# Blend stage of a two-layer graph network: a block's own h times its softmax weight, from GpSimd to ScalarE

## The chip, the core and the metric

One core of a Trainium2 chip runs the whole kernel in one launch. The metric is the device time in microseconds, the median of three runs. TensorE (PE) multiplies matrices, VectorE (DVE), ScalarE (ACT) and GpSimd (POOL) do elementwise work, SyncE (SP) issues loads and stores. Each engine runs its own instructions in the order written; they meet in semaphores alone.

## What is computed

12,500 nodes with 256 features, 200,000 edges sorted by target. The first layer is graph attention with 4 heads of 64 columns, with an edge from each node to itself; the second an equivariant convolution; each ends in a residual sum and a layer norm. Of the first layer the part that matters here:

```python
h = (x @ W).reshape(N, H, C)
alpha = jnp.exp(e - e_max[dst])
denom = jax.ops.segment_sum(alpha, dst, num_segments=N)
alpha = alpha / (denom[dst] + EPS)
msg = h[src] * alpha[:, :, None]
agg = jax.ops.segment_sum(msg, dst, num_segments=N)
out = jax.nn.elu(agg.reshape(N, H * C) + bias + x @ skip_W)
x1 = _layernorm(x + out)
```

The edge of a node to itself adds `exp(...)` times the node's own h to the sum. The kernel keeps that weight as `pself` (four numbers a node, one a head).

## The kernel before

Nodes are cut into NB = 98 blocks of 128, one node a partition. Four stages follow a preparation: edges of the first layer (its sums over the edges stay in `acc`, in SBUF), the blend stage (3057 to 3480 us of the span), edges of the second layer, and the last sum with its norm.

The blend stage is one loop over blocks, written as a `step_b(b, s, there)` for each engine and run by `steps(eng, n, lead, tail, step)`: step b is run for b from -lead to n + tail - 1, the first eight steps and the last ones written out, 88 steps in a hardware loop. In its step b an engine works on several blocks at once, `b + 2` to `b - 3`, and the order of the lines in the step is the order of work on that engine. Buffers of a block have TURN = 4 slots.

What each engine does in step b, in this order:

- SyncE: loads h, x and x transposed of block b + 3, stores the result of block b - 3.
- GpSimd (L549 to L562): waits for the three loads of block b + 2 and multiplies its h by `pself` (L554); adds `acc` (L558); then, after VectorE's variance of block b (L1243), raises it to the power -0.5 (L562).
- ScalarE: relu (L692) and exp (L695) of block b + 1, after VectorE's L1264; the two copies of block b - 2's products (L699, L700); the copy of block b - 1's transposes (L704), after TensorE's L912; the copy of block b - 2's rest `b_r` (L707), after VectorE's L1289 of this step.
- TensorE: products of block b - 2 (L899), the skip product of block b + 2 (L905 to L907), after VectorE's L1264, the transposes of block b - 1 (L912), after VectorE's second L1246.
- VectorE: waits for GpSimd's add of block b + 1 and multiplies by `rden`, the reciprocal of the denominator (L1254); block b's elu sum (L1259); block b + 1 plus the skip product (L1264); block b (L1267); first part of block b - 1's norm (L1246, needs GpSimd's power of block b - 1); statistics of b (L1275); second part of the norm (L1246); mean and variance of b (L1239, L1243); block b - 3's lowest part (L1284); block b - 2's rest (L1289, after ScalarE's L700).

`wait` puts a wait on the next instruction; `wait_apart` adds an empty instruction behind it.

Of the kernel before, what the change touches and what calls it, by code (L numbers as in the profile page):

```python
# [34 lines left out]
ALU = mybir.AluOpType  # L35
# [3 lines left out]
ds = bass.ds  # L39

P = 128
# [4 lines left out]
TURN = 4  # L46
# [10 lines left out]
def wait(eng, s, value):  # L57

    if not (isinstance(value, int) and value <= 0):
        eng.wait_ge(s, value)  # L60


def wait_apart(eng, s, value):

    if not (isinstance(value, int) and value <= 0):
        eng.wait_ge(s, value)
        eng.nop(nofuse=True)


def landed(g, slot, dmas=1):  # L70

    return dmas * (16 // TURN * g + 16 - 16 // TURN * slot)


def steps(eng, n, lead, tail, step):

    first, last = 2 * TURN, (n - lead) // TURN * TURN
    for g in range(-lead, first):  # L80
        step(g, g % TURN, lambda v: 0 <= v < n)
    with eng.Fori(first // TURN, last // TURN) as i:
        for slot in range(TURN):
            step(i * TURN + slot, slot, lambda v: True)
    for g in range(last, n + tail):
        step(g, g % TURN, lambda v: 0 <= v < n)


def bass_gat_equivariant_kernel(nc, x, xT, edges_sd, window_ends, ea8, ea4, W, WT, att_src, att_dst, bias, skip_W,
                                w1_s, w1_v, wsc_s, wsc_v, w2_s, w2_v, fc_w1, fc_w2, fc_w3, g_s, g_v, out,  # L90
                                n_nodes, n_edges):
    NB, NP, EW, T = sizes(n_nodes, n_edges)
    D = x.shape[1]
    H, C = att_src.shape
# [23 lines left out]
    with ExitStack() as ctx:  # L118
# [6 lines left out]
        def sems(prefix, names):  # L125
            return [sem(f"{prefix}_{n}") for n in names.split()]
# [51 lines left out]
        def cut_a(n, new_stage=False):  # L178
# [23 lines left out]
        pself = cut(NB * H).rearrange("p (b h) -> p b h", h=H)  # L202
        rden = cut(NB * H).rearrange("p (b h) -> p b h", h=H)
# [41 lines left out]
        b_h = cut_b(TURN * D, True).rearrange("p (s d) -> p s d", s=TURN)  # L245
# [8 lines left out]
        mv = sb("mv", [P, TURN, 4])  # L254
# [6 lines left out]
        mid = cut(2 * PAIR * 2 * D).rearrange("p (s k c u) -> p s k c u", s=2, k=PAIR, c=8)  # L261
# [32 lines left out]
         s_wev) = sems("a", "idx oh otp ots ad z p msg agg acc f1 t1 h1 f2 t2 h2 f3 wev")  # L294
        slots = "0 1 2 3"
        s_hg, s_otst, s_ea, s_sh, s_wst = (sems(f"a_{n}", slots) for n in ("hg", "otst", "ea", "sh", "wst"))
        (s_rden, s_bt, s_bsum, s_bskip, s_bv, s_bm, s_be, s_belu, s_bs, s_bmv, s_brstd, s_bx1, s_bxp, s_bxT, s_by,
         s_bout, s_br, s_bmid, s_blo) = sems(
            "b", "rden t sum skip v m e elu s mv rstd x1 xp xT y out r mid lo")
        s_bin, s_bst = sems("b_in", slots), sems("b_st", slots)  # L300
        (s_cy, s_csr, s_csame, s_cix, s_cpr, s_cmid, s_ccnt, s_cnum, s_cmt, s_cmT, s_coT, s_coTsb, s_co, s_cosb, s_csum, s_ccmb) = sems(
            "c", "y sr same ix pr mid cnt num mt mT oT oTsb o osb sum cmb")
        s_cw, s_cin, s_cpa, s_add = (sems(f"c_{n}", slots) for n in ("w", "in", "pa", "add"))
        (s_dsum, s_ddeg, s_ddn, s_do, s_dsq, s_dms, s_drs, s_dn, s_dz, s_dmv, s_drstd, s_dout) = sems(
            "d", "sum deg dn o sq ms rs n z mv rstd out")
        s_din, s_dx, s_dst = sems("d_in", slots), sems("d_x", slots), sems("d_st", slots)
# [30 lines left out]
        def _(sp):  # L337
# [108 lines left out]
            def step_c(u, s, there):  # L446
                if s % 2 == 0 and there(u + 4):
                    wait(sp, s_cy, u + 2)
                    sp.dma_start(c_ot[:, s // 2, :, :].rearrange("p k e -> p (k e)"), one(ot_tab, u // 2 + 2)
                                 ).then_inc(s_cin[s], 16)  # L450
                if s % 2 == 0 and there(u + 2):
                    q = (s + 2) % TURN
                    wait(sp, s_csr, u)
                    sp.dma_start(c_parts[:, q // 2, :].rearrange("w (k e) -> w k e", k=GROUP),
                                 src_tab[ds((u + 2) * PAIR, GROUP), :, :].rearrange("k w e -> w k e")
                                 ).then_inc(s_cpa[q], 16)
                n = (s + 3) % TURN
                if there(u + 3):
                    w = numbers(sp, window_row, (u + 3) * PAIR, PAIR, EW)
                    wait(sp, s_cmid, u)  # L460
                    for k in range(PAIR):
                        sp.dma_start(wt[:, n, k, :], one(wv, w[k])).then_inc(s_cw[n], 16)
# [24 lines left out]
        def _(pool):  # L487
            g = nc.gpsimd
# [58 lines left out]
            def step_b(b, s, there):  # L547
                n = (s + 2) % TURN
                if there(b + 2):  # L549
                    hs = b_h[:, n, :]  # L550
                    hs4 = hs.rearrange("p (h c) -> p h c", h=H)

                    wait_apart(pool, s_bin[n], landed(b + 2, n, 3))
                    g.tensor_tensor(hs4, hs4, pself[:, ds(b + 2, 1), :].rearrange("p o (h c) -> p (o h) c", c=1  # L554
                                                                                  ).to_broadcast([P, H, C]),
                                    ALU.mult).then_inc(s_bt, 1)
                    wait_apart(pool, s_bt, 2 * (b + 2) + 1)
                    g.tensor_tensor(hs, hs, acc[:, ds(b + 2, 1), 0:D].rearrange("p o d -> p (o d)"), ALU.add  # L558
                                    ).then_inc(s_bt, 1)
                if there(b):  # L560
                    wait(pool, s_bmv, 3 * (b + 1))
                    g.tensor_tensor(mv[:, s, 3:4], mv[:, s, 2:3], half[:, 0:1], ALU.pow).then_inc(s_brstd, 1)  # L562
# [41 lines left out]
        def _(act):  # L604
            a = nc.scalar
# [19 lines left out]
            for q in range(NQ):  # L625
                n = min(4, NC - 4 * q) * P
# [60 lines left out]
            def step_b(b, s, there):  # L687
                m, o, n = (s - 1) % TURN, (s - 2) % TURN, (s + 1) % TURN
                if there(b + 1):
                    wait(act, s_bv, b + 2)  # L690
                    wait(act, s_bs, b - 2)
                    a.activation(b_e[:, n, :], b_v[:, n, :], ACT.Relu, scale=-1.0).then_inc(s_bm, 1)  # L692
                if there(b + 1):
                    wait(act, s_bm, b + 2)
                    a.activation(b_e[:, n, :], b_e[:, n, :], ACT.Exp, scale=-1.0).then_inc(s_be, 1)  # L695
                if there(b - 2):
                    maps = PS[:, 3 + s % 2, :].rearrange("p (j m u) -> p j m u", j=2, m=2)
                    wait(act, s_by, b - 1)
                    a.copy(y3[:, ds(b - 2, 1), 0, :].rearrange("p o (j u) -> p (o j) u", j=2), maps[:, :, 0, :])  # L699
                    a.copy(b_x1[:, o, D:].rearrange("p (j u) -> p j u", j=2), maps[:, :, 1, :]).then_inc(s_bout, 1)  # L700
                if there(b - 1):
                    wait(act, s_bxp, b)
                    wait(act, s_by, b - 2)
                    a.copy(b_x1T[:, m % 2, :, :], PS[:, 2, 0:256].rearrange("p (k n) -> p k n", k=2)).then_inc(s_bxT, 1)  # L704
                if there(b - 2):
                    wait(act, s_br, b - 1)
                    a.copy(y3[:, ds(b - 2, 1), 1, :].rearrange("p o d -> p (o d)"), b_r[:, s % 2, :]).then_inc(s_bmid, 1)  # L707

            steps(act, NB, 1, 2, step_b)


            act.wait_ge(s_blo, NB)
# [51 lines left out]
        def _(pe):  # L764
# [9 lines left out]
            for c in range(-(-T // 512)):  # L774
                e = min(T, (c + 1) * 512)
                last = mm(PS[0:33, c, 0:e - c * 512], two[0:NB, :], stepm[:, c * 512:e], start=True, stop=True)
# [143 lines left out]
            def step_c(u, s, there):  # L920
                n, m, o = (s + 1) % TURN, (s - 1) % TURN, (s - 3) % TURN
# [47 lines left out]
                    count()  # L969
                if there(u + 1):  # L970
                    if n % 2 == 0:
                        wait(pe, s_cin[n], landed(u + 1, n))
                    wait(pe, s_cmid, u)
                    for k in range(PAIR):
                        for i in (2, 1, 0):
                            last = mm(PS[:, Y_BANK[n % 2], k * D:(k + 1) * D], c_ot[:, n // 2, n % 2 * PAIR + k, :],  # L976
                                      y3[:, ds(b[k], 1), i, :].rearrange("p o d -> p (o d)"),
                                      start=(i == 2), stop=(i == 0))
                    last.then_inc(s_cy, 1)
# [4 lines left out]
                        last = nc.tensor.transpose(PS[:, T_BANK[0], j * P:(j + 1) * P], oT_sb[:, j, :], ident[:, :])  # L984
                    last.then_inc(s_co, 1)
                if m % 2 == 0 and there(u - 1):
                    wait(pe, s_cpa[m], landed(u - 1, m))
                    wait(pe, s_csame, u - 1)
                    mm(PS[:, SR_BANK, :], ones_b, c_parts[:, m // 2, :], start=True, stop=True).then_inc(s_csr, 2)  # L989

# [18 lines left out]
        def _(dve):  # L1009
            v = nc.vector  # L1010
# [238 lines left out]
            def step_b(b, s, there):  # L1249
                n, m = (s + 1) % TURN, (s - 1) % TURN  # L1250
                if there(b + 1):
                    hs4 = b_h[:, n, :].rearrange("p (h c) -> p h c", h=H)
                    wait_apart(dve, s_bt, 2 * (b + 2))
                    v.tensor_tensor(hs4, hs4, rden[:, ds(b + 1, 1), :].rearrange("p o (h c) -> p (o h) c", c=1  # L1254
                                                                                 ).to_broadcast([P, H, C]),
                                    ALU.mult).then_inc(s_bsum, 1)
# [178 lines left out]
```

## Time and profile before

| | |
|---|---|
| median of 3 runs | 7266.64 us (7259.7 to 7271.49) |
| the profiled execution, its own time | 7338.37 us |
| its span | 7335.8 us |
| TensorE matmul busy | 6443.9 us, 88% |
| VectorE busy | 5231.9 us, 71% |
| GpSimd busy | 4802.6 us, 65% |
| ScalarE busy | 4207.1 us, 57% |
| granted TensorE clock, mean | 0.96 of full speed |

The busy shares are averages over stages with different limits; the change is in one stage of some 422 us, so the numbers of that stage alone count. An instruction's row names its line in the kernel, its output and input by the program's names (most tiles of this stage lie in one tensor, `arena`), partitions x elements, and in square brackets how long the engine had been idle and who released it. A granted clock of 1.00 is 2.4 GHz, 0.50 is 1.2 GHz.

### The profile page before, as it was taken

The page shows a single profiled execution, that of the slowest core. Times are in us where ns is not written, and L with a number is a line of the kernel's source. Part 1 is how long each engine was busy: PE and PEld are TensorE (multiplying, and loading weights), DVE is VectorE, ACT ScalarE, POOL GpSimd, SP SyncE. Part 2 cuts the span into 40 slices and gives each one's busy share as a digit, 9 for nine tenths or more (in the row PEclk, how much of TensorE's full clock was granted, in tenths as well). Part 3 has the DMA queues.
Part 4 walks back from the last instruction along what each step waited for, and adds up shares of the span by engine and source line. Part 5 has one row for each costly group of instructions (what it writes and reads, how often), then busy time and mean ns, then how long its engine had stood idle before and what let it go on. Part 6 is the DMA issues. An engine that isn't in the chain of part 4 may idle for free.

```text
span 7335.8 us, 210965 instructions
## 1 busy us (share of the span) xinstructions
PE 6443.9 (88%) x42774; PEld 4394.0 (60%) x42775; DVE 5231.9 (71%) x16784; ACT 4207.1 (57%) x11999; POOL 4802.6 (65%) x4057
## 2 busy tenths in 40 slices
PE   6778777777777777787999999999999999999976
PEld 5444444444444444454777777777777777777754
DVE  3666666667666666799777777777777777777779
ACT  2444444444444444444677777777777777777732
POOL 3555555555555555454677777777777777777778
PEclk8998999999999999888999999999999999999999
DMA  5677777777777777644788888888888888888899
GB/s 181 184 194 197 197 194 193 196 195 197 196 199 193 196 197 196 184 155 147 134 141 140 141 139 141 139 141 139 141 140 140 140 140 141 139 141 139 141 238 300
DMA packets 1213481, 1244.70 MB, mean 170 GB/s; under 512 B 216576, under 2 KB 1124737, under 8 KB 1213345
## 3 DMA queue, kind: packets, MB, share of 16 engines
q0 software_dynamic: 328176, 468.28, 39.5%
q1 hardware_dynamic: 885266, 776.00, 36.4%
q8 instruction: 13, 0.21, 0.0%
q14 instruction: 26, 0.21, 0.0%
HBM read 641.49 MB, written 602.17 MB: 170 GB/s over the span
## 4 chain that ended last, share of the span: by engine, by line
PE 54%; issue 18%; SPq 17%; POOL 4%; DVE 3%; another core or an unknown queue 2%; DMA 1%; ACT 1%; DVEq 1%; POOLq 0%; ACTq 0%
PE PS L929 12%; PE PS L957 12%; PE PS L939 10%; PE PS L976 8%; SPq L398 7%; PE PS L984 5%; SPq L409 2%; PE PS L852 2%; SPq L405 2%; SPq L401 2%; SPq L395 2%; PE PS L989 2%; POOL arena L558 1%; PE PS L842 1%
## 5 line engine op out<-in xcount | busy, mean ns | idle before, releaser
L577 POOL DMA_INDIRECT part<-arena,c_idx x1664 | 2658.4, 1598 | 911.2 <-issue 522.3
L538 POOL DMA_INDIRECT big<-h_tab,big x1664 | 1647.3, 990 | 1217.1 <-PE PS L852 598.0
L852 PE MATMUL PS<-big 128*128 128x260 f32 x3328 | 1092.2, 439 | 387.3 <-DVE big L1172 257.1
L1172 DVE TENSOR_TENSOR big<-big,PS 128x260 f32 x1664 | 701.8, 422 | 684.7 <-PE PS L852 429.8
L1310 DVE TENSOR_TENSOR arena<-PS,arena 128x384 f32<-128x384 f32 x832 | 463.9, 558 | 987.2 <-PE PS L976 958.3
L852 PEld LDWEIGHTS PS<-big 128*128 128x128 f32 x3328 | 580.6, 203 | 760.9 <-issue 653.7
L929 PEld LDWEIGHTS PS<-ident,arena 128*128 128x128 f32 x6656 | 714.4, 141 | 500.3 <-issue 497.7
L929 PE MATMUL PS<-ident,arena 128*128 128x128 f32 x6656 | 909.6, 280 | 2.0 <-DVE arena L1333 2.0
L957 PE MATMUL PS<-arena,w2m 128*64 128x128 f32 (+1 forms) x6656 | 903.3, 392 | 0.0
L722 ACT COPY arena<-PS 128x512 f32<-128x512 f32 x1664 | 894.2, 589 | 10.8 <-PE PS L929 10.4
L939 PE MATMUL PS<-arena 128*128 128x256 f32 x3328 | 856.5, 380 | 1.1 <-ACT arena L744 1.1
L727 ACT COPY arena<-PS 128x512 f32<-128x512 f32 x832 | 488.7, 587 | 452.0 <-issue 373.1
L976 PE MATMUL PS<-big,arena 128*128 x4992 | 681.3, 272 | 4.9 <-DMA arena<-ot_tab 4.9
L652 ACT ACTIVATE big<-PS,arena 128x128 f32<-128x128 f32 x1664 | 513.2, 360 | 230.5 <-PE PS L842 149.6
L1164 DVE TENSOR_TENSOR big<-big 128x256 f32<-128x256 f32 x1664 | 638.7, 423 | 0.0
L682 ACT COPY big<-PS 128x512 bf16<-128x512 bf16 x416 | 244.6, 588 | 680.4 <-remote 558.6
L939 PEld LDWEIGHTS PS<-arena 128*128 128x128 f32 x3328 | 567.7, 191 | 44.5 <-ACT arena L744 2.0
L739 ACT COPY arena<-PS 128x512 f32<-128x512 f32 x832 | 488.0, 587 | 178.7 <-ACT c_num L735 103.3
L842 PE MATMUL PS<-arena 64*128 64x256 f32 x3328 | 540.1, 448 | 0.8 <-ACT big L654 0.8
L871 PE MATMUL PS<-arena 16*128 16x256 f32 x832 | 298.7, 439 | 252.2 <-DMA arena<-in_ea 135.2
L744 ACT COPY arena<-PS 128x512 f32<-128x512 f32 x832 | 486.9, 585 | 54.9 <-PE PS L984 19.5
L984 PE MATMUL PS<-ident,arena 128*128 128x128 f32 x3328 | 499.8, 273 | 0.0
(182 smaller groups left out, 11029.3 us busy)
## 6 DMA issues: line engine op xcount, KB each, us to landing
w_tab<-big SPq DMA_DIRECT2D x416, 520.0 KB
arena<-w_tab SPq DMA_DIRECT2D x1664, 130.0 KB
part<-arena SPq DMA_DIRECT2D x1664, 32.1 KB
ot_tab<-big SPq DMA_DIRECT2D x416, 128.0 KB
arena<-ot_tab SPq DMA_DIRECT2D x416, 128.0 KB
arena<-part SPq DMA_DIRECT2D x392, 128.5 KB, 3.5
big<-h_tab,big POOLq DMA_INDIRECT x1664
part<-arena,c_idx POOLq DMA_INDIRECT x1664
```

What stands on the lines that cost most here:

```text
L538: pool.indirect_dma_start(hg[:, s, k, :], None, h_tab, bass.IndirectOffsetOnAxis(ap=sidx[:, s, k:k + 1], axis=0)).then_inc(s_hg[s], 16)
L577: pool.indirect_dma_start(part[q], bass.IndirectOffsetOnAxis(ap=c_idx[:, s, k:k + 1], axis=0), o_cmb[:, s, k, :], None, compute_op=ALU.add ...
L722: a.copy(midT[:, k, :, :], PS[:, T_BANK[k], :].rearrange("p (c e) -> p c e", c=4)).then_inc(s_cmT, 1)
L842: last = mm(PS[:, 4 + i, k * D:(k + 1) * D], h2[i * MUL:(i + 1) * MUL, o % 2, k * P:(k + 1) * P], fc3[i * MUL:(i + 1) * MUL, :], start=Tru ...
L852: mm(PS[:, 2 + k % 2, 0:HW], oh[:, p, k, :], hg[:, p, k, :], start=True, stop=True).then_inc(s_agg, 1)
L929: last = nc.tensor.transpose(PS[:, T_BANK[k], j * P:(j + 1) * P], mid[:, m % 2, k, 2 * j:2 * j + 2, :].rearrange("p c u -> p (c u)"), iden ...
L939: last = mm(PS[:, SUM_BANK, k * D:(k + 1) * D], same[:, o, k, :], o_sb[:, k, :], start=True, stop=True)
L957: last = mm(PS[k * MUL:(k + 1) * MUL, OT_BANK, first * P:(first + n_comps) * P], w2m[:, min(first, 1), :], midT[:, k, first:first + n_comp ...
L976: last = mm(PS[:, Y_BANK[n % 2], k * D:(k + 1) * D], c_ot[:, n // 2, n % 2 * PAIR + k, :], y3[:, ds(b[k], 1), i, :].rearrange("p o d -> p ...
L984: last = nc.tensor.transpose(PS[:, T_BANK[0], j * P:(j + 1) * P], oT_sb[:, j, :], ident[:, :])
L1164: v.tensor_tensor(x, x, hg[:, o, k, D:HW].rearrange("p (h o) -> p h o", o=1).to_broadcast([P, H, C]), ALU.mult).then_inc(s_msg, 1)
L1172: v.tensor_tensor(x, x, PS[:, 2 + k % 2, 0:HW], ALU.add).then_inc(s_acc, 1)
```

## The change

GpSimd's multiply by `pself` goes. ScalarE does it at the end of its step b, for block b + 2, as four multiplies of 128x64, one a head, each with the weight as a [128, 1] scale operand; a new semaphore `self` tells GpSimd, whose add waits for it. ScalarE's `lead` goes from 1 to 2, so that blocks 0 and 1 are served too. `s_bt` now counts one a block. To make room for the semaphore, two sets of four in the second edge stage become sets of two (only the even ones were in use).

```diff
@@ semaphores
-        (s_rden, s_bt, s_bsum, s_bskip, s_bv, s_bm, s_be, s_belu, s_bs, s_bmv, s_brstd, s_bx1, s_bxp, s_bxT, s_by,
+        (s_rden, s_bself, s_bt, s_bsum, s_bskip, s_bv, s_bm, s_be, s_belu, s_bs, s_bmv, s_brstd, s_bx1, s_bxp, s_bxT, s_by,
...
-        s_cw, s_cin, s_cpa, s_add = (sems(f"c_{n}", slots) for n in ("w", "in", "pa", "add"))
+        s_cw, s_add = sems("c_w", slots), sems("c_add", slots)
+        s_cin, s_cpa = sems("c_in", "0 1"), sems("c_pa", "0 1")
...
@@ GpSimd, step_b
                 if there(b + 2):
                     hs = b_h[:, n, :]
-                    hs4 = hs.rearrange("p (h c) -> p h c", h=H)
-
-                    wait_apart(pool, s_bin[n], landed(b + 2, n, 3))
-                    g.tensor_tensor(hs4, hs4, pself[:, ds(b + 2, 1), :].rearrange("p o (h c) -> p (o h) c", c=1
-                                                                                  ).to_broadcast([P, H, C]),
-                                    ALU.mult).then_inc(s_bt, 1)
-                    wait_apart(pool, s_bt, 2 * (b + 2) + 1)
+                    wait_apart(pool, s_bself, b + 3)
                     g.tensor_tensor(hs, hs, acc[:, ds(b + 2, 1), 0:D].rearrange("p o d -> p (o d)"), ALU.add
                                     ).then_inc(s_bt, 1)
@@ ScalarE, step_b
                 if there(b - 2):
                     wait(act, s_br, b - 1)
                     a.copy(y3[:, ds(b - 2, 1), 1, :].rearrange("p o d -> p (o d)"), b_r[:, s % 2, :]).then_inc(s_bmid, 1)
-
-            steps(act, NB, 1, 2, step_b)
+                if there(b + 2):
+                    q = (s + 2) % TURN
+                    wait(act, s_bin[q], landed(b + 2, q, 3))
+                    for h in range(H):
+                        last = a.mul(b_h[:, q, h * C:(h + 1) * C], b_h[:, q, h * C:(h + 1) * C],
+                                     pself[:, ds(b + 2, 1), h:h + 1].rearrange("p o h -> p (o h)"))
+                    last.then_inc(s_bself, 1)
+
+            steps(act, NB, 2, 2, step_b)
@@ VectorE, step_b
                 if there(b + 1):
                     hs4 = b_h[:, n, :].rearrange("p (h c) -> p h c", h=H)
-                    wait_apart(dve, s_bt, 2 * (b + 2))
+                    wait_apart(dve, s_bt, b + 2)
```

## Rows read from the trace of the kernel before

**Rows 1.** Busy time by stretch, the whole stage; us (instructions), then PEclk, DMA, GB/s.
```profile
3057.40:3479.50 422.10, 343.83 (x1176) 215.29 (x1176) 382.51 (x1078) 207.75 (x588) 213.84 (x294) 0.86 0.48 151
```

**Rows 2.** Busy time by stretch, two stretches of 10 us in the loop.
```profile
3100.00:3110.00 10.00, 7.86 (x32) 5.30 (x32) 9.92 (x28) 5.07 (x15) 6.05 (x9) 1.00 0.58 186
3280.00:3290.00 10.00, 8.70 (x22) 5.34 (x20) 8.84 (x26) 4.20 (x12) 6.01 (x9) 0.57 0.55 169
```

**Rows 3.** Line L554: durations ns min/median/max, first and last start.
```profile
L554 POOL TENSOR_TENSOR arena<-arena x98: 607/612/894, 3057.4 to 3461.3; 128x256 f32<-128x256 f32 x98
```

**Rows 4.** Groups by line, 3097 to 3460 us: busy, mean ns, idle before.
```profile
L558 POOL TENSOR_TENSOR arena<-arena,big 128x256 f32<-128x256 f32 x87 | 74.4, 855 | 20.1 <-POOL arena L554 20.1
L562 POOL TENSOR_TENSOR mv<-mv,half 128x1 f32<-128x1 f32 x86 | 60.5, 703 | 152.3 <-DVE mv L1243 152.3
L1267 DVE SCALAR_TENSOR_TENSOR arena<-arena 128x256 f32<-128x256 f32 x87 | 53.9, 620 | 0.0
L1259 DVE SCALAR_TENSOR_TENSOR arena<-arena 128x256 f32<-128x256 f32 x87 | 53.0, 609 | 0.0
L1254 DVE TENSOR_TENSOR arena<-arena 128x256 f32<-128x256 f32 x86 | 48.5, 564 | 3.0 <-POOL arena L554 1.1 <-issue 0.3
```

**Rows 5.** Order of time (start, duration, us), VectorE, undisturbed by GpSimd.
```profile
3176.38 0.42 DVE L1254 TENSOR_TENSOR arena<-arena 128x256 f32<-128x256 f32 x1
3177.05 0.42 DVE L1264 TENSOR_TENSOR arena<-arena,PS 128x256 f32<-128x256 f32 x1
3179.07 0.43 DVE L1284 TENSOR_TENSOR big<-arena,big 128x256 f32 x1
```

**Rows 6.** Order of time, the power beside VectorE, ahead of the loop.
```profile
3069.47 0.69 POOL L562 TENSOR_TENSOR mv<-mv,half 128x1 f32<-128x1 f32 x1 [1.63 <-DVE mv L1243]
3069.66 0.42 DVE L1259 SCALAR_TENSOR_TENSOR arena<-arena 128x256 f32<-128x256 f32 x1
```

**Rows 7.** Groups by line, ScalarE, whole span: busy, mean ns, idle before.
```profile
L652 ACT ACTIVATE big<-PS,arena 128x128 f32<-128x128 f32 x1664 | 513.2, 360 | 230.5 <-PE PS L842 149.6 <-issue 48.0 <-remote 32.5
L704 ACT COPY arena<-PS 128x256 f32<-128x256 f32 x98 | 36.5, 372 | 98.0 <-PE PS L912 98.0
L755 ACT ACTIVATE arena<-arena 128x64 f32<-128x64 f32 x98 | 25.1, 256 | 217.4 <-DVE d_n L1363 135.4 <-DVE arena L1359 82.0
```

**Rows 8.** Order of time, VectorE and ScalarE: distances and one hop.
```profile
3177.61 0.41 ACT L707 CAST big<-arena 128x256 f32 x1
3177.91 0.42 ACT L692 ACTIVATE arena<-arena 128x256 f32<-128x256 f32 x1
...
3263.70 0.42 DVE L1284 TENSOR_TENSOR big<-arena,big 128x256 f32 x1
3264.05 0.42 DVE L1289 TENSOR_TENSOR arena<-PS,big 128x256 f32<-128x256 f32 x1
3264.58 0.41 ACT L707 CAST big<-arena 128x256 f32 x1 [0.26 <-DVE arena L1289]
```

**Rows 9.** Order of time, TensorE's path to L704 at the full clock.
```profile
3178.73 0.60 PE L905 MATMUL PS<-arena 128*128 128x256 f32 x2
3180.31 0.44 PE L912 MATMUL PS<-ident,arena 128*128 128x128 f32 x2
3180.79 0.37 ACT L704 COPY arena<-PS 128x256 f32<-128x256 f32 x1 [1.12 <-PE PS L912]
```

**Rows 10.** Order of time, the stage's start: add and VectorE's first instruction.
```profile
3058.18 0.72 POOL L558 TENSOR_TENSOR arena<-arena,big 128x256 f32<-128x256 f32 x1
3059.00 0.42 DVE L1254 TENSOR_TENSOR arena<-arena 128x256 f32<-128x256 f32 x1 [9.45 <-POOL arena L558]
```

**Rows 11.** Order of time, the same path of TensorE at the lower clock.
```profile
3168.90 1.06 PE L905 MATMUL PS<-arena 128*128 128x256 f32 x2
3171.89 0.69 PE L912 MATMUL PS<-ident,arena 128*128 128x128 f32 x2
3172.62 0.37 ACT L704 COPY arena<-PS 128x256 f32<-128x256 f32 x1 [2.74 <-PE PS L912]
```

More of the change, by code:

```diff
@@ L296, in bass_gat_equivariant_kernel @@
         s_hg, s_otst, s_ea, s_sh, s_wst = (sems(f"a_{n}", slots) for n in ("hg", "otst", "ea", "sh", "wst"))
-        (s_rden, s_bt, s_bsum, s_bskip, s_bv, s_bm, s_be, s_belu, s_bs, s_bmv, s_brstd, s_bx1, s_bxp, s_bxT, s_by,
+        (s_rden, s_bself, s_bt, s_bsum, s_bskip, s_bv, s_bm, s_be, s_belu, s_bs, s_bmv, s_brstd, s_bx1, s_bxp, s_bxT, s_by,
          s_bout, s_br, s_bmid, s_blo) = sems(
-            "b", "rden t sum skip v m e elu s mv rstd x1 xp xT y out r mid lo")
+            "b", "rden self t sum skip v m e elu s mv rstd x1 xp xT y out r mid lo")
         s_bin, s_bst = sems("b_in", slots), sems("b_st", slots)
@@ L449, in step_c @@
                     sp.dma_start(c_ot[:, s // 2, :, :].rearrange("p k e -> p (k e)"), one(ot_tab, u // 2 + 2)
-                                 ).then_inc(s_cin[s], 16)
+                                 ).then_inc(s_cin[s // 2], 16)
                 if s % 2 == 0 and there(u + 2):
@@ L455, in step_c @@
                                  src_tab[ds((u + 2) * PAIR, GROUP), :, :].rearrange("k w e -> w k e")
-                                 ).then_inc(s_cpa[q], 16)
+                                 ).then_inc(s_cpa[q // 2], 16)
                 n = (s + 3) % TURN
@@ L971, in step_c @@
                     if n % 2 == 0:
-                        wait(pe, s_cin[n], landed(u + 1, n))
+                        wait(pe, s_cin[n // 2], landed(u + 1, n))
                     wait(pe, s_cmid, u)
@@ L986, in step_c @@
                 if m % 2 == 0 and there(u - 1):
-                    wait(pe, s_cpa[m], landed(u - 1, m))
+                    wait(pe, s_cpa[m // 2], landed(u - 1, m))
                     wait(pe, s_csame, u - 1)
```

## The prediction

> **What bounds the stage now.** The change touches only the blend stage, so I first cut the trace to that stage with the view of busy time by stretch. From its first GpSimd multiply to its last VectorE step it takes 422.10 us of the span; VectorE is busy for 382.51 us of them, TensorE for 343.83, GpSimd for 213.84, ScalarE for 207.75 [rows 1]. The reader is to see that VectorE is the bound and ScalarE has half its time free. In a stretch at the full clock VectorE is busy for 9.92 of 10 us; where the granted clock is 0.57, near its lower level of 1.2 GHz, TensorE is busy for 8.70 and VectorE falls to 8.84 [rows 2]. So there are two regimes: VectorE sets the step at the full clock, TensorE at the lower one.
>
> One step a block. GpSimd's multiply L554 starts 98 times, first at 3057.4 and last at 3461.3 us, so a step is 403.9 / 97 = 4.16 us [rows 3].
>
> Then the groups of instructions by line in the loop. The multiply that is moved (L554) takes 612 ns in the median [rows 3], the add behind it (L558) 855 in the mean, the power (L562) 703, and GpSimd waits 152.3 us in 86 times, 1.8 us a step, for VectorE's L1243 [rows 4]. GpSimd has slack now because its multiply and add work one whole step ahead: in its step b it makes block b + 2, VectorE takes that block as the first thing of step b + 1, and GpSimd is released for it already by the variance of step b - 1. This slack is what I follow through the change.
>
> **What is removed.** One GpSimd instruction a block. It also slows VectorE today: L1254, L1259 and L1267, which have two inputs in SBUF, take 564, 609 and 620 ns in the mean [rows 4], while L1254 takes 0.42 us in a step that GpSimd leaves alone [rows 5]. So the two tensor operations of GpSimd cost VectorE up to 0.14 + 0.19 + 0.20 = 0.53 us a step. The power costs it nothing: L1259 beside it takes 0.42 us [rows 6].
>
> **What is added, and where it lies.** Four ScalarE multiplies of 128x64 a block. None of this shape is in the trace. A 128x64 activation from SBUF without a pointer operand takes 256 ns; a 128x128 from PSUM with one takes 360, while a 128x256 copy from PSUM without one takes 372; from 256 ns at 64 columns to the 0.42 us of L692 at 256 a column is worth 0.85 ns, so the pointer is worth 360 - (372 - 128 x 0.85) = 97 ns [rows 7, 8]. So one multiply takes about 0.35 us. A ScalarE instruction of 0.41 us is followed by the next after 0.30 [rows 8], an overlap of 0.11: four take 3 x 0.24 + 0.35 = 1.07 us. Bounds: 3 x 0.15 + 0.26 = 0.69 without a price for the pointer, and 4 x 0.35 = 1.40 without overlap. I take 1.07. As mere load this would be free: ScalarE has 207.75 / 98 = 2.1 us a block now, and 3.2 would still be under 4.16.
>
> But the four stand at the end of ScalarE's step b, behind the copy L707, which waits for VectorE's L1289, the last instruction of VectorE's step b. GpSimd's add waits for the four (and its power is now queued behind that add), and VectorE's step b + 1 begins with L1254, which waits for this add. Nothing of VectorE's next step can start before; everything else of VectorE is queued behind L1254. The work that was a step ahead becomes a loop of one step:
> L1254 to L1289 on VectorE, then L707, four multiplies, the add, and L1254 again.
>
> **The step after, at the full clock**, from the start of L1254, with the times of a step in which GpSimd does not disturb VectorE. L1264 starts at 3177.05 - 3176.38 = 0.67 and ends at 1.09; L1284 starts at 2.69 [rows 5]. The end of L1289 comes 3264.05 - 3263.70 + 0.42 = 0.77 later, at 3.46, and L707 starts 0.11 after that, at 3.57 [rows 8]. The other path to L707 is TensorE's: its L905 waits for L1264, so 1.20 with the same hop, then 1.58 to the transposes L912 and 0.48 more to the copy L704 [rows 9], 3.26, and L707 behind it (0.37 less the overlap of 0.11) no earlier than 3.52. A tie; I take 3.57. From L707 to the next instruction 0.30, the four 1.07: 4.94. The hop to the add: 20.1 us in 87 times between multiply and add today [rows 4], 0.23, gives 5.17. The add without contention takes 0.72 [rows 10]: 5.89. The hop to L1254 was 0.10 in the part written out ahead of the loop [rows 10]; inside the loop VectorE works out an address between, so I take 0.23 as for the other hop: 6.12 us. Lower bound with 0.69 for the four and 0.10 for both hops: 5.48. Upper bound with 1.40: 6.45. The power, queued behind the add, starts with L1254 and takes 0.7 us, while its reader is VectorE's fifth instruction, 4 x 0.67 / 2 = 1.3 us in [rows 5]: hidden, with 0.5 us to spare.
>
> **At the lower clock** TensorE's path is the long one: from L905 to L912 2.99 us, to L704 0.73 [rows 11], so L704 at 4.92, L707 0.26 later at 5.18 instead of 3.57, and the step 7.73 us.
>
> **The sum.** A granted clock of 0.86 over the stage [rows 1] is 28% of the time at half rate. TensorE's work a step stays the same, in a longer step, so nothing says that this share falls; I take 28%: 6.12 + 0.28 x 1.61 = 6.57 us. Blocks for which both L1289 and the multiplies exist in ScalarE's step: 2 to 95, so 94 steps. 94 x (6.57 - 4.16) = 227 us. The profiled execution took 7338.37 us, 72 above the median of 7266.64; the difference is far smaller than the span and I add it to the median unscaled (1% of it would be 2 us): 7493. The semaphores of two loads of the edge stage behind, cut from four to two each, keep their counts (only two of the four were ever used) and cost nothing.
>
> **Rules of the Trainium skill.** GPSIMD Engine Reference, Specifications: GpSimd shares its SBUF interfaces with VectorE and contends with VectorE instructions that have two SBUF inputs. By that rule, the trace agrees (0.53 us a step above), and alone it would make the change a gain. TensorE: Matmul & The Clock Gate, Why this matters for your kernels: no long idle gap of TensorE, no throughput drop. By it the new step, whose longest gap is some 2.5 us, would stay at 2.4 GHz and the step 6.12 us, the time 7451; the trace speaks against it, with 0.57 where TensorE was busy 8.70 of 10 us [rows 2].
>
> **Rivals.**
> 1. The clock is low for most of the stage, because TensorE is busy for only about 0.786 x 4.1 = 3.2 of 6.1 us [rows 2]. For it: the granted clock falls at times already where TensorE is more than three quarters busy. Against: at the lower clock its work grows as 2.99 to 1.58 [rows 9, 11], to 6.0 of 7.7 us, about the share at which it has the full clock now. 94 x (7.73 - 4.16) = 336 us: 7602.
> 2. A gain: the multiplies find a place before VectorE needs them, and VectorE is relieved of contention. 94 x -0.53 = -50 us: 7217. It decides at one point: whether block b + 2's add is done before L1289 of step b ends. For it: ScalarE's free half and the contention rows. Against it: the order written out, in which ScalarE reaches the multiplies only after L1289.
> 3. A chain, but with hops and multiplies cheaper than my lower bound, such as 5.1 us a step: 94 x 0.94 = 88 us, 7355.
> 4. No change: a chain that costs just what contention gives back, a step of about 4.2 us. It would need L1289's end to L1254 in 4.16 - 3.46 = 0.7 us, which the 0.72 of the add alone uses up.
>
> **How the numbers follow.** The forecast (a step of 5.48 to some 7.1 us, 7391 to 7543) has 0.73, rival 1 0.15, rival 3 0.06, rival 2 0.04, rival 4 0.02. Range: from just above the lower bound, 7395, to just beyond rival 1, 7610. Differences of 0.2% (15 us) are about what a measurement of this kernel tells from none: faster 0.04, same 0.02, slower 0.94.
>
> **What would show it.** Right: VectorE's L1254 idle for about 2.5 us a step, released by L558; ScalarE's L707 directly after L1289, four multiplies of about 0.35 us behind it; L1259 and L1267 back at 0.42; VectorE's share in the stage down from 0.91 to about 0.6; the stage some 650 us long. Wrong: no idle time ahead of L1254 (rival 2), a granted clock near 0.5 (rival 1), or a wait of GpSimd's add for the loads instead of for ScalarE.

## The result and the profile after

| | before | after |
|---|---|---|
| median of 6 runs | 7265.87 us (7254.32 to 7271.49) | 7447.43 us (7443.14 to 7448.74) |
| ratio | | 1.0252, 95% interval 1.0239 to 1.0265 |
| span of the profiled execution | 7335.8 us | 7440.3 us |

The change costs 182 us. The whole of it lies in the blend stage. The two views below (busy time by stretch; columns as in [rows 1]) cut it in both kernels from VectorE's first to its last multiply by `rden`; first the kernel before, then the one after.

```profile
3059.00:3465.30 406.30, 332.20 (x1152) 208.30 (x1150) 373.68 (x1052) 201.18 (x569) 211.04 (x290) 0.88 0.49 153
```

```profile
2983.30:3575.40 592.10, 479.50 (x1155) 288.25 (x1154) 326.36 (x1051) 297.91 (x959) 118.60 (x193) 0.61 0.34 105
```

406.3 us became 592.1, so 185.8 more. VectorE's work fell from 373.7 to 326.4 us and it is busy for 55% of the stage instead of 92; GpSimd's fell by 92 us, ScalarE's rose by 97. The granted clock is 0.61, most of the stage at 1.2 GHz. The spans of the two profiled executions differ by only 104.5 us, because the same code ahead of the stage took 75.7 us less in the second one (2983.3 against 3059.0), and the code behind it 5.6 less; hence the comparison by stage. That the semaphores of the edge stage behind cost nothing, as forecast, agrees with it.

The page of the kernel after, its row of the granted clock in 40 slices, shows the stage as the three sixes:

```profile
PEclk8999999999999999666899999999999999999999
```

What VectorE waits for, by the view of one line (L1256 after is L1254 before; "98" is how often):

```profile
L1256 DVE TENSOR_TENSOR arena<-arena x98: 424/426/427, 2983.3 to 3575.4; 128x256 f32<-128x256 f32 x98
L1256 DVEq FUSED_REGOPS  x88: 76/76/88, 3031.9 to 3569.3; - x88
  POOL arena L553: 265.7, 98
```

VectorE waits 2.7 us a block, each time for GpSimd's add (L553; L558 in the kernel before). Before it was almost nothing, 3.0 us in all [rows 4]. Within the loop a step takes (3569.3 - 3031.9) / 87 = 6.18 us. Most of its steps take 6.11 to 6.14 us and about every fourth 6.31; the first nine of the stage, ahead of the loop, take 3.92 to 6.01, which brings the mean of all 97 to 6.10. The groups by line in the loop (after L1261, L1269 are before L1259, L1267; L707 are the new multiplies, L557 the power; some rows left out, here as in all such lists):

```profile
L707 ACT ACTIVATE arena<-arena 128x64 f32<-128x64 f32 x300 | 79.5, 335 | 0.0
L553 POOL TENSOR_TENSOR arena<-arena,big 128x256 f32<-128x256 f32 x75 | 54.4, 725 | 370.7 <-ACT arena L707 370.7
L557 POOL TENSOR_TENSOR mv<-mv,half 128x1 f32<-128x1 f32 x75 | 41.2, 549 | 0.0
L1256 DVE TENSOR_TENSOR arena<-arena 128x256 f32<-128x256 f32 x75 | 31.9, 425 | 200.4 <-POOL arena L553 200.4
L1269 DVE SCALAR_TENSOR_TENSOR arena<-arena 128x256 f32<-128x256 f32 x74 | 31.0, 419 | 0.0
L1261 DVE SCALAR_TENSOR_TENSOR arena<-arena 128x256 f32<-128x256 f32 x75 | 31.4, 418 | 0.0
```

The add takes 725 ns instead of 855, and VectorE's three instructions with two inputs in SBUF are at 425, 419 and 418 ns instead of 564, 620 and 609 [rows 4]: the contention is gone, and with it nothing is won, since VectorE now stands still while GpSimd adds.

One whole step in order of time, at 1.2 GHz (L1248 is VectorE's L1246 of before, L914 TensorE's L912, L699 and L702 ScalarE's L704 and L707; rows left out):

```profile
3216.95 1.06 PE L907 MATMUL PS<-arena 128*128 128x256 f32 x2
3217.58 0.42 DVE L1256 TENSOR_TENSOR arena<-arena 128x256 f32<-128x256 f32 x1 [2.67 <-POOL arena L553]
3218.26 0.41 DVE L1266 TENSOR_TENSOR arena<-arena,PS 128x256 f32<-128x256 f32 x1
3218.79 1.22 PE L909 MATMUL PS<-arena 1*128 1x256 f32 x2
3219.48 0.51 DVE L1248 TENSOR_SCALAR arena<-arena,mv 128x192 f32<-128x192 f32 x1
3220.05 0.69 PE L914 MATMUL PS<-ident,arena 128*128 128x128 f32 x2
3220.62 0.42 DVE L1291 TENSOR_TENSOR arena<-PS,big 128x256 f32<-128x256 f32 x1
3220.77 0.37 ACT L699 COPY arena<-PS 128x256 f32<-128x256 f32 x1 [0.67 <-PE PS L914]
3221.16 0.41 ACT L702 CAST big<-arena 128x256 f32 x1
3221.47 1.06 ACT L707 ACTIVATE arena<-arena 128x64 f32<-128x64 f32 x4
3222.76 0.73 POOL L553 TENSOR_TENSOR arena<-arena,big 128x256 f32<-128x256 f32 x1 [4.89 <-ACT arena L707]
3223.70 0.42 DVE L1256 TENSOR_TENSOR arena<-arena 128x256 f32<-128x256 f32 x1 [2.66 <-POOL arena L553]
```

The reader is to see the ring: L1256 at 3217.58, VectorE's last instruction L1291 ending at 3221.04, the copy L702 at 3221.16, the four multiplies at 3221.47 for 1.06 us, the add at 3222.76, and L1256 again at 3223.70, 6.12 us later. And one thing that the prediction did not have: TensorE's skip product (L907) starts at 3216.95, ahead of VectorE's step, not behind its L1266.

The step is as long where more of it runs at the full clock. By the view of busy time by stretch, the step above and one with a granted clock of 0.84:

```profile
3217.58:3223.70 6.12, 5.61 (x13) 3.30 (x13) 3.42 (x11) 3.11 (x10) 1.23 (x3) 0.50 0.33 107
3310.23:3316.34 6.11, 5.31 (x17) 2.88 (x16) 3.41 (x11) 3.11 (x10) 1.22 (x3) 0.84 0.36 107
```

Divided in this way at each start of L1256, the stage has 58 steps wholly at 1.2 GHz and 39 with a clock between 0.68 and 0.93; the median of either group is 6.13 us.

### The profile page after: what moved, and what is told of

Read it like the earlier page. It is cut to its first block, busy times and chain, and to the rows that moved or that the text cites. A ratio compares the mean times of both kernels' runs of the same rounds, so it can differ in the third digit from the quotient of the medians.

```text
span 7440.3 us, 211425 instructions
## 1 busy us (share of the span) xinstructions
PE 6538.8 (88%) x42774; PEld 4439.5 (60%) x42775; DVE 5163.0 (69%) x16784; ACT 4295.5 (58%) x12391; POOL 4824.0 (65%) x3959
## 4 chain that ended last, share of the span: by engine, by line
PE 55%; issue 15%; SPq 12%; DVE 6%; another core or an unknown queue 3%; POOL 3%; ACT 2%; DMA 1%; DVEq 1%; POOLq 0%; ACTq 0%
PE PS L931 11%; PE PS L959 11%; PE PS L941 10%; PE PS L978 8%; SPq L399 5%; PE PS L986 5%; PE PS L854 3%; PE PS L991 2%; SPq L402 2%; SPq L406 2%; SPq L410 2%; SPq L396 1%; PE PS L844 1%; PE PS L795 1%
## 5 line engine op out<-in xcount | busy, mean ns | idle before, releaser
L572 POOL DMA_INDIRECT part<-arena,c_idx x1664 | 2724.3, 1637 | 841.0 <-issue 641.3
L539 POOL DMA_INDIRECT big<-h_tab,big x1664 | 1695.2, 1019 | 1093.7 <-issue 397.6
L844 PE MATMUL PS<-arena 64*128 64x256 f32 x3328 | 517.4, 433 | 0.8 <-ACT big L649 0.8
L1323 DVE TENSOR_TENSOR arena<-arena 128x384 f32<-128x384 f32 x832 | 456.2, 548 | 0.0
```

Source lines behind the costliest of these rows:

```text
L539: pool.indirect_dma_start(hg[:, s, k, :], None, h_tab, bass.IndirectOffsetOnAxis(ap=sidx[:, s, k:k + 1], axis=0)).then_inc(s_hg[s], 16)
L572: pool.indirect_dma_start(part[q], bass.IndirectOffsetOnAxis(ap=c_idx[:, s, k:k + 1], axis=0), o_cmb[:, s, k, :], None, compute_op=ALU.add ...
L844: last = mm(PS[:, 4 + i, k * D:(k + 1) * D], h2[i * MUL:(i + 1) * MUL, o % 2, k * P:(k + 1) * P], fc3[i * MUL:(i + 1) * MUL, :], start=Tru ...
```

## The experiments

All ratios are to the kernel before, run beside the versions in the same set; that kernel's median was 7271, 7309 and 7328 us in the three sets, so versions of different sets are compared by ratio or by the length of the stage. The length of the stage is always from VectorE's first to its last multiply by `rden`; divided by 97 it is the mean step.

### Where the multiplies stand in ScalarE's step

The same instructions at three earlier places of the step, everything else as in the changed kernel. The last line of each diff is what they stand ahead of.

```diff
@@ first_in_step
+                if there(b + 2):
+                    ... wait for the loads, four multiplies of block b + 2, inc s_bself
                 if there(b + 1):
                     wait(act, s_bv, b + 2)
@@ before_transposes_copy
+                if there(b + 2):
+                    ...
                 if there(b - 1):
                     wait(act, s_bxp, b)
@@ before_rest_copy
+                if there(b + 2):
+                    ...
                 if there(b - 2):
                     wait(act, s_br, b - 1)
```

> The four ScalarE multiplies of block b + 2 stand at the start of ScalarE's step b, ahead of the relu, instead of at its end; nothing else differs from the changed kernel. Chain theory (the multiplies wait for VectorE's last instruction of the step, and VectorE's next step waits for them): the block is ready more than 1 us before VectorE takes it, the idle time ahead of VectorE's multiply by rden goes from 2.7 us a step to about none, VectorE is the bound again at the full clock with a step of 3.6 to 3.9 us, and the kernel takes 7225 to 7260 us, no slower than before. Load theory (four small instructions with a pointer operand are too much for ScalarE): it stays within 10 us of the changed kernel's 7447. Clock theory (TensorE at 1.2 GHz is what made the stage long): the time follows the granted clock in the stage; if that stays near 0.6 the kernel stays near 7440.

> The four multiplies stand between the two copies of the products and the copy of the transposes. Chain theory: the loop is now VectorE's step up to its third instruction, relu, exp, two copies, four multiplies, add: 2.51 + 2.24 = 4.75 us a step at the full clock, against 6.12, and about 6.0 at 1.2 GHz, where TensorE's own work is as long; the mean lies at 5.0 to 5.5 and the kernel at 7350 to 7395 us. Load theory: 7447 within 10. Clock theory: it follows the granted clock.

> The four multiplies stand directly ahead of the last copy of ScalarE's step, behind the copy of the transposes. Chain theory: they no longer wait for VectorE's last instruction but for TensorE's transposes: 3.21 + 2.24 = 5.45 us a step at the full clock and about 6.0 at 1.2 GHz; the mean at 5.5 to 6.0, the kernel at 7390 to 7435 us, between the changed kernel and the position ahead of the transposes' copy. Load theory: 7447 within 10.

| place of the multiplies | ratio (95%) | median, us | stage, us | step, us | granted clock in the stage |
|---|---|---|---|---|---|
| end of the step (the change) | 1.0252 (1.0239 to 1.0265) | 7447.4 | 592.1 | 6.10 | 0.61 |
| ahead of the rest's copy | 1.0201 (1.0184 to 1.0218) | 7416.5 | 546.1 | 5.63 | 0.70 |
| ahead of the transposes' copy | 1.0081 (1.0061 to 1.01) | 7326.5 | 460.2 | 4.74 | 0.80 |
| first in the step | 0.9918 (0.9904 to 0.9932) | 7212.9 | 346.7 | 3.57 | 0.97 |

The stage's rows, in the order rest's copy, transposes' copy, first:

```profile
2998.20:3544.30 546.10, 428.86 (x1155) 265.12 (x1154) 326.14 (x1051) 287.56 (x959) 118.59 (x193) 0.70 0.36 114
```

```profile
2988.10:3448.30 460.20, 372.56 (x1155) 232.94 (x1154) 326.86 (x1052) 283.41 (x959) 118.67 (x193) 0.80 0.43 135
```

```profile
3007.20:3353.90 346.70, 294.78 (x1151) 189.59 (x1150) 323.58 (x1051) 281.55 (x957) 137.31 (x193) 0.97 0.57 179
```

ScalarE does the same multiplies in all of them (281 to 298 us busy), so they are not too much for it: the load theory is out. All four have ScalarE's longer lead and the new semaphores as well, so these do not make the change slow. Each place moves the time by what it takes out of the ring. Ahead of the rest's copy the time, 7416.5 us, lies in the stated band (7390 to 7435). For the place ahead of the transposes' copy 4.75 us were worked out at the full clock; its 34 steps there take 4.66 in the median, and that the mean of all is 4.74 is in part luck. Its time lies 24 us under the stated band, because I had mixed in steps of 6.0 us at 1.2 GHz, and its 13 steps at that clock take 4.75 in the median. First in the step, the ring is open, and the version beats the kernel before by 0.8%: 58 us. That is more than was expected (7225 to 7260), and its cause is followed up below.

### Half of the multiplies

```diff
-                    for h in range(H):
+                    for h in range(2):
```

> The changed kernel with two multiplies instead of four: heads 2 and 3 are not multiplied by their weight. Chain theory: each multiply lies on the loop with its distance to the next, 0.24 us, so 94 x 0.48 = 45 us less than the changed kernel: 7402, within 10. Clock theory: less than 10 us of difference.

Median 7418.8 us, 29 less than with four multiplies and 7 above the stated band. But the kernel before took 5 us more in this set, and by the ratio, 1.0196 (1.0179 to 1.0213), the difference is 0.56% or 41 us. The stage took 551.5 us: 40.6 us less than with four, 0.43 us a step where 0.48 were expected. The 69 steps with a granted clock above one half take 5.65 us in the median, 0.48 less than 6.13; the 28 at 1.2 GHz take 5.85, which fits TensorE's own loop at that clock (see below). So each multiply's distance to the next does lie on the ring.

### The wait alone

The kernel before, nothing moved, one wait more on GpSimd ahead of its own multiply:

```diff
+                    wait(pool, s_bmid, b - 1 if there(b - 2) else 0)
                     wait_apart(pool, s_bin[n], landed(b + 2, n, 3))
```

> The kernel before with one wait more: GpSimd, ahead of its multiply of block b + 2, waits for ScalarE's last copy of step b (the copy of block b - 2's rest). No work is moved. Chain theory: the same loop as in the changed kernel, with the copy's whole 0.41 us and GpSimd's multiply of 0.61 us in place of ScalarE's 0.30 + 1.07 and its hop: 3.5 to 3.6 + 0.11 + 0.41 + 0.1 + 0.61 + 0.23 + 0.72 + 0.23 = 5.9 to 6.05 us a step, and the kernel takes 7430 to 7450 us though ScalarE does no multiply. Load theory (the four ScalarE instructions cost the time): within 10 us of the kernel before.

Ratio 1.0250 (1.0234 to 1.0266), against 1.0252 for the change; stage 586.8 us. The median, 7494.6 us, is above the band, but in this set the kernel before took 7309 too: 185 us less. The mean step is 6.05 us. Order of time:

```profile
3201.16 0.72 POOL L559 TENSOR_TENSOR arena<-arena,big 128x256 f32<-128x256 f32 x1 [0.23 <-POOL arena L555]
3202.10 0.43 DVE L1255 TENSOR_TENSOR arena<-arena 128x256 f32<-128x256 f32 x1 [2.63 <-POOL arena L559]
...
3205.69 0.40 ACT L708 CAST big<-arena 128x256 f32 x1
3206.42 0.61 POOL L555 TENSOR_TENSOR arena<-arena 128x256 f32<-128x256 f32 x1 [4.02 <-ACT big L708]
```

The add, and VectorE 0.94 us after its start; then, at the end of VectorE's step, the copy L708 and GpSimd's multiply that waits for it, 0.73 us after its start (0.51 was expected). This is the run that settles the cause: the whole loss comes with the dependence, without a single multiply on ScalarE. The multiply is on the ring here too, but on GpSimd, with its 0.61 us.

### TensorE's clock

```diff
                     mm(PS[:, n % 2, 0:D], ones[0:1, :], brow[:, :], start=False, stop=True).then_inc(s_bskip, 1)
+                    mm(PS[:, 5, 0:D], ident[:, :], wm[:, 0, :, :].rearrange("p m u -> p (m u)"), start=True, stop=True)
```

> The changed kernel with one matmul more in each of TensorE's steps, 128x256 from constants into an unused bank, behind the skip product; its result is read by nobody. Chain theory: TensorE waits there anyway, so the granted clock of the stage rises from 0.61 and the time stays within 10 us of 7447. Clock theory (the low clock is a cause of the long step): the time falls with the rising clock, by 50 us or more if it reaches 0.9.

Median 7523.0 us, ratio 1.0287 (1.0271 to 1.0302): slower than the change by 0.35%, so neither theory's number. The granted clock of the stage rose from 0.61 to 0.69, and the time rose too. By itself this run would not clear the low clock, since TensorE also had more to do. But its four steps of the loop at a granted clock of 1.00 take 6.12 to 6.13 us, the same as the changed kernel's steps at 0.50: the low clock is not what makes the change slow. Why the time was not the same shows in VectorE's first instruction of six successive steps and in two stretches, one step at a mixed clock and some two steps at the lower one:

```profile
3150.95 0.43 DVE L1257 TENSOR_TENSOR arena<-arena 128x256 f32<-128x256 f32 x1 [2.68 <-POOL arena L553]
3157.07 0.43 DVE L1257 TENSOR_TENSOR arena<-arena 128x256 f32<-128x256 f32 x1 [2.67 <-POOL arena L553]
3163.92 0.42 DVE L1257 TENSOR_TENSOR arena<-arena 128x256 f32<-128x256 f32 x1 [3.39 <-POOL arena L553]
3170.90 0.43 DVE L1257 TENSOR_TENSOR arena<-arena 128x256 f32<-128x256 f32 x1 [3.52 <-POOL arena L553]
3178.03 0.42 DVE L1257 TENSOR_TENSOR arena<-arena 128x256 f32<-128x256 f32 x1 [3.51 <-POOL arena L553]
3184.17 0.42 DVE L1257 TENSOR_TENSOR arena<-arena 128x256 f32<-128x256 f32 x1 [2.68 <-POOL arena L553]
```

```profile
3150.95:3157.09 6.14, 3.68 (x10) 2.42 (x10) 3.44 (x12) 3.11 (x10) 1.25 (x3) 0.65 0.34 107
3163.25:3177.00 13.75, 12.40 (x28) 7.50 (x28) 6.84 (x22) 6.01 (x20) 2.20 (x4) 0.50 0.31 95
```

The steps are 6.12, 6.85, 6.98, 7.13 and 6.14 us. At 0.50 TensorE is busy for 12.40 of 13.75 us: with the matmul added, its own loop at 1.2 GHz is longer than the ring. Without it, it just fits. How long it is shows in a step of the kernel before, which has no ring, at the lower clock:

```profile
3237.80:3243.82 6.02, 5.56 (x14) 3.29 (x12) 3.51 (x13) 2.06 (x6) 3.08 (x5) 0.50 0.41 130
```

It takes 6.02 us, as do the longest others of that kernel, against the ring's 6.12. That the lower clock cost the change nothing hangs on this tenth of a microsecond.

### Where the gain of the best version comes from

First the removal alone: the kernel before without GpSimd's multiply.

```diff
-                    g.tensor_tensor(hs4, hs4, pself[...].to_broadcast([P, H, C]), ALU.mult).then_inc(s_bt, 1)
-                    wait_apart(pool, s_bt, 2 * (b + 2) + 1)
```

> The kernel before without GpSimd's multiply by the weight; nothing does it instead, so a block's own h enters with weight one. It measures what the removal alone gives. Contention theory: VectorE's share of the 0.53 us a step that belongs to this multiply comes back, 0.15 to 0.4 us a step, and the kernel takes 7225 to 7250 us; if it reaches the 7213 of the version with the multiplies first in the step, ScalarE's four multiplies cost nothing there.

Ratio 0.9974 (0.9964 to 0.9985), median 7293.0 us against 7309.3, stage 392.5 us: far less than the best version's gain, 13.8 us of the stage against 59.6, and with 0.14 us a step just under what was expected (0.15 to 0.4). Groups by line in the loop (L554 is the add, L1250 and L1255 VectorE's first two instructions):

```profile
L554 POOL TENSOR_TENSOR arena<-arena,big 128x256 f32<-128x256 f32 x75 | 59.2, 790 | 0.0
L1255 DVE SCALAR_TENSOR_TENSOR arena<-arena 128x256 f32<-128x256 f32 x75 | 48.7, 650 | 0.0
L1250 DVE TENSOR_TENSOR arena<-arena 128x256 f32<-128x256 f32 x75 | 45.8, 611 | 2.2 <-issue 0.8
```

The add alone still takes 0.19 + 0.23 us a step from those two, because it now starts where the multiply started, beside them. So I asked where GpSimd's work lies, not how much it is. The same kernel, and the kernel before, each with a wait for ScalarE's relu, which moves GpSimd's work some 1.8 us into VectorE's step:

```diff
+                    wait(pool, s_bm, b + 2 if there(b + 1) else 0)
                     wait_apart(pool, s_bin[n], landed(b + 2, n, 3))
```

> The same wait in the kernel without GpSimd's multiply by the weight (a block's own h enters with weight one; nothing does the multiply). Placement theory: the add starts about 1.7 us into VectorE's step, where it does not meet the three instructions; 0.990 to 0.994 of before instead of 0.997, the same as with ScalarE's four multiplies, which therefore cost nothing there. Removal theory: 0.997 as without the wait.

> The kernel before with one wait more: GpSimd, ahead of its multiply of block b + 2, waits for ScalarE's relu in step b; no work is moved. The multiply then starts about 1.7 us into VectorE's step and the add at 2.6, beside VectorE's instructions with one SBUF input or one from PSUM, and the add ends 3.5 us in with its hop, just when VectorE can start its next step (3.4 to 3.5). Placement theory (what VectorE loses depends on which of its instructions GpSimd's two meet): VectorE's three instructions go back to 0.42 us, the step falls to 3.5 to 3.7 us, and the kernel gets as fast as the version with ScalarE's multiplies, 0.990 to 0.995 of before. Removal theory (only taking the multiply from GpSimd helps): no faster than before, or slower by the wait.

> The version with the four multiplies first in ScalarE's step, once more, beside the two runs that follow on the same chip: 0.989 to 0.994 of the kernel before, the granted clock of the stage near 1, VectorE's three instructions with two SBUF inputs at 0.42 us.

| | ratio (95%) | stage, us | clock |
|---|---|---|---|
| no multiply, add waits for the relu | 0.9918 (0.9904 to 0.9931) | 347.3 | 0.97 |
| ScalarE's multiplies first, once more | 0.9914 (0.9901 to 0.9928) | 346.6 | 0.97 |
| kernel before, GpSimd waits for the relu | 0.9975 (0.9964 to 0.9987) | 396.1 | 0.89 |

Groups by line of the first and of the third:

```profile
L555 POOL TENSOR_TENSOR arena<-arena,big 128x256 f32<-128x256 f32 x97 | 70.5, 727 | 198.3 <-ACT arena L689 198.3
L1251 DVE TENSOR_TENSOR arena<-arena 128x256 f32<-128x256 f32 x98 | 41.0, 418 | 14.1 <-POOL arena L555 8.5 <-issue 5.6
L1256 DVE SCALAR_TENSOR_TENSOR arena<-arena 128x256 f32<-128x256 f32 x96 | 40.3, 419 | 0.0
```

```profile
L559 POOL TENSOR_TENSOR arena<-arena,big 128x256 f32<-128x256 f32 x97 | 83.8, 864 | 22.1 <-POOL arena L555 20.8
L1285 DVE TENSOR_TENSOR big<-arena,big 128x256 f32 x88 | 56.0, 636 | 4.1 <-issue 3.8
L1255 DVE TENSOR_TENSOR arena<-arena 128x256 f32<-128x256 f32 x98 | 41.0, 419 | 34.5 <-POOL arena L559 34.5
```

A wait added to the kernel without the multiply is worth 45 us of the stage and brings it to the version that does the multiply on ScalarE: in that place ScalarE's four cost nothing, and the gain is that the add no longer meets VectorE's L1251 and L1256 (418 and 419 ns). With GpSimd's own multiply in front, the add comes too late: it meets L1285, which has two SBUF inputs as well (636 ns instead of 425), and VectorE waits 34.5 us for it. That was expected as equal to the best version and is not; behind the relu there is no room for both on GpSimd. Order of time in the best version:

```profile
3202.42 0.41 DVE L1256 TENSOR_TENSOR arena<-arena 128x256 f32<-128x256 f32 x1
3202.93 1.06 ACT L688 ACTIVATE arena<-arena 128x64 f32<-128x64 f32 x4
3204.22 0.73 POOL L553 TENSOR_TENSOR arena<-arena,big 128x256 f32<-128x256 f32 x1 [2.03 <-ACT arena L688]
3204.31 0.52 DVE L1248 TENSOR_SCALAR arena<-arena,mv 128x192 f32<-128x192 f32 x1
3204.75 0.17 DVE L1241 BATCH_NORM_AGGREGATE mv<-stat 128x2 f32<-128x6 f32 x1
3205.78 0.41 DVE L1256 TENSOR_TENSOR arena<-arena 128x256 f32<-128x256 f32 x1
```

The multiplies end at 3203.99, the add lies beside L1248 and L1241, which have one tensor input, and VectorE takes the block at 3205.78, 0.83 us after the add's end. The steps at the full clock went from 4.06 us in the mean, in the kernel before, to 3.54: 0.52 a step, some 50 of the 59.6 us. The rest goes with the clock: all but 5 of the best version's 97 steps have the full clock, against 73 in the kernel before.

## Why the prediction held, and where it did not

**The ring: right.** Order of work, not amount of work. The seven terms beside the step shown above: VectorE's part 3.46 expected, 3.46 measured; hop to the copy 0.11 and 0.12; copy to the first multiply 0.30 and 0.31; four multiplies 1.07 and 1.06; hop to the add 0.23 and 0.23; the add 0.72 and 0.73; hop to VectorE 0.23 and 0.21. The sum is 6.12 in both. The power behind the add is hidden, as stated: in that step it ends at 3217.87, and L1248, which needs it, starts at 3218.92.

**What is removed: right, and worth nothing here.** The three instructions went back to 0.42 us as forecast, but not by the removal alone: without the multiply and with the add in its old order, two of them stayed at 0.61 and 0.65.

**The step at the lower clock: wrong.** I put TensorE's skip product behind VectorE's L1264 of the same step. It waits for `s_bv` at b + 1, which is block b, done one step earlier (the "after VectorE's L1264" in the list of the engines' steps means the step before): the trace has it at 3216.95, ahead of VectorE's step. TensorE is then done with the skip product at 3220.01, just when VectorE's L1248 ends, at 3219.99. The transposes follow at 3220.05, their copy L699 at 3220.77, and the copy L702 behind it starts 0.12 us after VectorE's last instruction, as at the full clock. The step is 6.12 at 1.2 GHz, not 7.73. That it is no longer than at the full clock is a near thing: TensorE's own loop of 6.02 us happens to be just shorter than the ring. The row of the kernel before on which I rested the 7.73 [rows 11] is right; what I joined it to is not.

**The share of the lower clock: wrong.** I carried over 28% on the ground that nothing spoke for another share; a granted clock of 0.61 is 78% of the stage at half rate. Rival 1's condition came true and its price did not.

**The sum.** The term 0.28 x 1.61 = 0.45 us a step, 42 us, was not there. Without it the prediction reads 7266.64 + 94 x (6.12 - 4.16) = 7451 us; measured 7447.43. The forecast of 7493 was too high by this one term, and the range down to 7395 held. That the two errors, a price of 1.61 us a step and a share of 28%, came to only 42 us is luck: with the measured share of 78% the same price would have added 118 us. It is in part luck too that 7451 is so near, since the steps of the loop are longer than 6.12 in the mean and the first ones shorter. Between the ends that gave 422.10 before, the stage took 606.8 us, where some 650 were stated, for the same reason as the forecast. VectorE's share, 0.55, is not the stated 0.6 either, but that figure never followed from the rest: (382.51 - 50) / 650 is 0.51. Nor does a step of "some 7.1 us", the forecast's upper end, come out of its terms, which give 6.45 + 0.45 = 6.90.

**The rules of the Trainium skill.** The Trainium skill, GPSIMD Engine Reference, Specifications, names contention of GpSimd with VectorE's instructions that have two SBUF inputs. The runs agree in detail: beside GpSimd's add L1250 and L1255, and in another version L1285, are slowed, while L1248 and L1241 are not. The Trainium skill, TensorE: Matmul & The Clock Gate, Why this matters for your kernels, says that throughput does not drop as long as TensorE has no long idle gap. The 7451 worked out by it is nearest to the result, but not for its reason: the clock did fall, to 0.61 with TensorE busy for 479.5 of 592.1 us and never idle for more than 2.64 us. That the time is the same comes from TensorE's path being no longer than the ring.

**Rival 2 named the right point.** It asked whether block b + 2's add is done before L1289 of step b ends. With the multiplies first in the step it is, and the version takes 7212.9 us against the 7217 worked out for it; part of that agreement is luck: the contention came back in full, as it counted, but it counted no gain from the clock, and the kernel before ran 5 us longer in this set.

## What to carry to other kernels

When work of one step ahead is moved to another engine, read the place where it lands in that engine's order: what the engine waits for just ahead of it, and whether the reader is the one that releases this wait. Here a move that was free as load turned a pipeline into a ring and cost 2.5%; the same four lines at the start of the step gain 0.8%. And before an engine is relieved, ask which of its neighbour's instructions it meets: taking the multiply from GpSimd alone shortened the stage by 14 us, and moving the add that was left by 1.8 us by another 45.

## What the runs showed of the hardware

- One GpSimd add of 128x256 beside VectorE's two-SBUF-input instructions costs VectorE 0.42 us a step (611 and 650 ns against 418 and 419). Beside instructions with one tensor input in SBUF it costs nothing that shows: L1248 takes 0.52 us and L1241 0.17 beside it, 0.51 and 0.17 in the changed kernel, where GpSimd stands still then.
- The granted clock of the stage went with the mean step although TensorE's instructions were the same: 0.97 at a step of 3.57 us, 0.88 at 4.19 (the kernel before), 0.80 at 4.74, 0.70 at 5.63, 0.61 at 6.10. Why is not shown here.
- A ScalarE multiply of 128x64 with a [128, 1] scale from SBUF took 335 ns, and four in a row 1.06 us, in the loop (at 3221.47), where the trace shows register work of 46 ns ahead of each, and in the part written out ahead of it (at 2981.31) alike.
